# Out-of-range rows for the empty places of the order by destination in a four-layer graph network

## The reference, cut to what matters

```python
x = _layernorm(x + _L0_gnn_ref(x, edge_index, edge_weight, weights))  # 3 hops: segment_sum(w * z[dst], src), 4 matmuls
x = _layernorm(x + _L1_gnn_ref(...))  # 8 heads; keys and values by edge type; softmax over the edges of each dst
x = _layernorm(x + _L2_gnn_ref(...))  # 4 heads; leaky_relu(x_l[src] + x_r[dst]); softmax over the edges of each dst
x = _layernorm(x + _L3_gnn_ref(...))  # 8 heads; softmax over the edges of each src, then summed over each dst
```

## Time and profile before

| | us |
|---|---|
| median of 3 runs (lowest, highest) | 9730.03 (9727.62, 9735.21) |
| the profiled execution's own time | 9737.26 |
| its span in the trace | 9735.5 |
| POOL, DVE, PE, ACT busy | 6993.0, 6539.5, 6374.2, 2118.1 |
| mean granted clock of TensorE, share of full | 0.686 |

### The profile page before, as it was taken

One profiled execution on the slowest core, in us unless ns is written; L12 is line 12 of the kernel. 1 busy time (PEld: TensorE's weight loads), 2 busy tenths in 40 slices (PEclk: granted clock), 3 DMA queues, 4 the chain that ended last, 5 costly groups with the idle time before them and its releaser, 6 DMA issues. The chain is left out here.

```text
span 9735.5 us, 171552 instructions
## 1 busy us (share of the span) xinstructions
PE 6374.2 (65%) x37681; PEld 5551.4 (57%) x37682; DVE 6539.5 (67%) x22695; ACT 2118.1 (22%) x6216; POOL 6993.0 (72%) x7418
## 2 busy tenths in 40 slices
PE   6777655547666577639404666767776688876666
PEld 5666544436655566634204666556675578766665
DVE  7555566668777777736305888877777666667777
ACT  5222100001111111112101222232222222223333
POOL 7777777767777777777776777547775577767775
PEclk7555555556666655569756888889999665667777
DMA  0000012122212212234303333222222322223333
GB/s 25 2 2 2 18 53 52 53 61 53 53 53 55 57 53 53 53 77 146 100 2 86 104 104 104 87 47 55 55 55 55 100 54 54 54 72 108 108 108 97
DMA packets 436037, 614.74 MB, mean 63 GB/s; under 512 B 176561, under 2 KB 312069, under 8 KB 435109
## 3 DMA queue, kind: packets, MB, share of 16 engines
q0 software_dynamic: 257024, 486.93, 19.6%
q1 hardware_dynamic: 178305, 119.49, 4.3%
q10 hardware_dynamic: 292, 3.41, 0.1%
HBM read 520.17 MB, written 89.19 MB: 63 GB/s over the span
## 5 line engine op out<-in xcount | busy, mean ns | idle before, releaser
L1179 PE MATMUL hop_sums<-hop_rows,hop_weighted 128*128 x4992 | 1152.1, 403 | 1053.2 <-SPq L1315 674.4
L1128 POOL DMA_INDIRECT hop_rows<-hops,k_src_gather x1568 | 1483.3, 946 | 486.8 <-issue 477.6
L1179 PEld LDWEIGHTS hop_sums<-hop_rows,hop_weighted 128*128 128x128 f32 x4992 | 989.6, 295 | 1158.8 <-issue 1158.7
L1505 POOL DMA_INDIRECT l_pass_rows<-left_table,k_dst_other x832 | 796.2, 957 | 433.2 <-issue 244.6
L1505 POOL DMA_INDIRECT l_pass_rows<-related,k_dst_typed x832 | 788.6, 948 | 308.6 <-issue 238.7
L1505 POOL DMA_INDIRECT l_pass_rows<-key_table,k_src_gather x784 | 744.3, 949 | 365.9 <-issue 234.8
L2000 POOL DMA_INDIRECT l_weigh_rows<-row_table,l_weigh_ring x832 | 790.0, 949 | 297.9 <-issue 213.1
L728 POOL DMA_INDIRECT src_sorted<-src_scatter_records,src_scatter_places x784 | 753.1, 961 | 260.4 <-issue 188.2
L1355 POOL DMA_INDIRECT dst_sorted<-rec,dst_places x768 | 752.8, 980 | 237.2 <-issue 237.2
L1128 POOL DMA_INDIRECT hop_rows<-in_x,k_src_gather x784 | 742.4, 947 | 249.0 <-issue 238.7
L1213 DVE TENSOR_SCALAR hop_weighted<-k_numbers,k_src_place,src_weight 128x128 f32<-128x128 f32 x2496 | 850.1, 403 | 15.7 <-issue 8.7
(11 more groups left out here) (477 smaller groups left out, 17048.9 us busy)
## 6 DMA issues: line engine op xcount, KB each, us to landing
related<-l_tables_rows SPq DMA_DIRECT2D x50, 1024.0 KB, 4.5
hop_rows<-hops,k_src_gather POOLq DMA_INDIRECT x1568
l_pass_rows<-related,k_dst_typed POOLq DMA_INDIRECT x832
l_pass_rows<-left_table,k_dst_other POOLq DMA_INDIRECT x832
l_weigh_rows<-row_table,l_weigh_ring POOLq DMA_INDIRECT x832
src_sorted<-src_scatter_records,src_scatter_places POOLq DMA_INDIRECT x784, 2.1
hop_rows<-in_x,k_src_gather POOLq DMA_INDIRECT x784, 2.5
dst_sorted<-rec,dst_places POOLq DMA_INDIRECT x784
```

What stands on the lines that cost most here:

```text
L1128: nc.gpsimd.indirect_dma_start(rows[:, s * G + g, :], None, table_in, bass.IndirectOffsetOnAxis(ap=o.gather[:, c:c + 1], axis=0),).then_in ...
L1179: last = nc.tensor.matmul(sums[:, b, g, :], weighted[:, s % SLOTS, g, :], rows[:, bass.ds(slots[g], 1), :], start=True, stop=True)
L1505: nc.gpsimd.indirect_dma_start(rows[:, s, g, :], None, table, bass.IndirectOffsetOnAxis(ap=index[:, c:c + 1], axis=0),).then_inc(got[s], 16)
```

## The change

The records of "no edge" now name source `NO_NODE` = 6,271, a row behind the last node, and type 7. The gathers of the three stages carry a bound: an index greater than it is not an error, and its row is not transferred. The bound is 6,249 for layer 2 and weighing, and 7 x 6,400 + 6,249 for layer 1. The first gathers into each ring slot (the first 11, 15 and 4 groups) carry no bound and transfer all 128 rows, row 6,271 for the empty places; later an empty place keeps what the ring slot held. The 352 entries with source 0 and type 0 are below the bound and are transferred as before. The gathers of layer 3's softmax get the new argument too, with no bound. In weighing GpSimd's first round is written out ahead of a loop of 51.

```diff
-PAD_STEP, PAD_SKIP = 7, 3
-assert PAD_STEP * (CH - 1) + PAD_SKIP * (P - 1) < N
+NO_NODE = NP - 1
+assert NO_NODE >= N
@@ load_beside
-        nc.gpsimd.iota(pad[:, :, 1], [[PAD_STEP, CH]], base=0, channel_multiplier=PAD_SKIP,
-                       allow_small_or_imprecise_dtypes=True).then_inc(filled, 1)
         nc.gpsimd.memset(pad[:, :, 0:1], -1.0).then_inc(filled, 1)
-        nc.gpsimd.memset(pad[:, :, 2:4], 0.0).then_inc(filled, 1)
+        nc.gpsimd.memset(pad[:, :, 1:2], float(NO_NODE)).then_inc(filled, 1)
+        nc.gpsimd.memset(pad[:, :, 2:3], float(TYPES - 1)).then_inc(filled, 1)
+        nc.gpsimd.memset(pad[:, :, 3:4], 0.0).then_inc(filled, 1)
...
-        act.wait_ge(filled, 3)
+        act.wait_ge(filled, 4)
@@ softmax_pass(..., ringed=False, last_row=None)
                     nc.gpsimd.indirect_dma_start(rows[:, s, g, :], None, table,
                                                  bass.IndirectOffsetOnAxis(ap=index[:, c:c + 1], axis=0),
-                                                 ).then_inc(got[s], 16)
+                                                 bounds_check=last_row if n >= ring else None,
+                                                 oob_is_err=False).then_inc(got[s], 16)
@@ weigh_and_sum
-            with pool.Fori(0, ROUNDS) as i:
+            def a_round(i, first):
...
-                                                     ).then_inc(got[s], 16)
+                                                     bounds_check=None if first else N - 1,
+                                                     oob_is_err=False).then_inc(got[s], 16)
+
+            in_rounds(pool, ROUNDS, a_round)
@@ the calls
+ layer 1: last_row=(TYPES - 1) * NPD + N - 1
+ layer 2: last_row=N - 1
```

More of the change, by code:

```diff
@@ L1361, in softmax_pass @@
 def softmax_pass(nc, k, o, index, table, row, head, values_at, spread, att, peaks, total, reload, loops, wg, name, beside=(),
-                 ringed=False):
+                 ringed=False, last_row=None):
     heads = D // head
@@ L3266, in graph_network @@
             softmax_pass(nc, k, by_dst, by_dst.typed, related.rearrange("t n f -> (t n) f"), 2 * D, D // HEADS1, D,
-                         k.x, None, False, total, (k.x[:], x_home), None, 4, "l1_pass")
+                         k.x, None, False, total, (k.x[:], x_home), None, 4, "l1_pass", last_row=(TYPES - 1) * NPD + N - 1)
             relation_output(nc, k, total, a["L1_gnn_w_basis_a"], a["L1_gnn_loop_weight"], a["L1_gnn_bias"], mix,
@@ L3283, in graph_network @@
             softmax_pass(nc, k, by_dst, by_dst.other, left_table, D + HEADS2, D // HEADS2, 0, right, att_row[:], True, total,
-                         None, (left, loop_scores, k.x[:], bias2[:]), 8, "l2_pass")
+                         None, (left, loop_scores, k.x[:], bias2[:]), 8, "l2_pass", last_row=N - 1)
             attention_output(nc, k, total, loop_scores, left_table, "l2_out")
```

## The result

The changed kernel takes 9832.4 us (median of 4 runs, 9824.3 to 9838.7) against 9732.6 us for the kernel before in the same runs: ratio 1.0104, 95% interval 1.0092 to 1.0116. It is slower by 100 us. The profiled execution took 9838.7 us with a span of 9837.0, 101.5 us longer than before.

The account below looks back on a forecast made before the run. POOL's (GpSimd's) time per gather instruction, not bytes, was taken as the bound. Check cost less freed rows less waits gave +21.3 (layer 1), +45.4 (layer 2), +20.3 (weighing): +87 us, forecast 9817 us, range 9660 to 10,080.

Parts of the forecast that it names:

- The case: Forecast case: in the three bounded stages the check costs more than left-out rows free; 9817 us, chance 0.40.
- the bound on 2,376 gathers: Comparing 128 indices per bounded gather on POOL: 80.4 us in layer 1, 78.7 in layer 2, 83.2 in weighing.
- left-out rows: POOL time freed by rows not transferred: 22.4 us in layer 1, 22.1 in layer 2, 22.6 in weighing.
- POOL's idle time filled: POOL's present waits shrink before a stage grows: 36.7 us in layer 1, 11.2 in layer 2, 40.3 in weighing.
- I take 102 ns: Assumed extra POOL time per bounded gather, taken from the smallest memset, as one more pass over one column.
- 85 ns for one more read command: Alternative price per bounded gather if the core writing the other descriptors reads indices too; sum +46 us, not +87.
- I take half, 3.7 ns: Assumed POOL time freed per left-out row, half of its full share of 7.4 ns in a 949 ns gather.
- a pair of descriptors for each piece moved: Rule behind the rival of a free check and left-out rows freeing POOL time: 9649 or 9680 us, chance 0.32.
- less the wait of 36.7: Layer 1's sum: 80.4 less 22.4, less POOL's whole wait of 36.7 us for VectorE, gives +21.3 us.
- The prediction's case of 40 ns: At about 40 ns a gather, nothing freed, layer 1 and weighing hide the cost; layer 2 pays 20 us.
- Named signs: Expected in the changed profile: bounded gathers about 1,045 ns, last 22 shorter, POOL's waits near zero, VectorE's weighing wait above 191.4.
- The edits at nothing: Three memsets for the fill (1.6 us at most, covered) and weighing's written-out first round were said to cost nothing.

## Why the prediction was right

The forecast was 9817 in a range of 9660 to 10,080; 9832 came. The case was the right one, and its place too: POOL's gathers with a bound, three stages, nothing elsewhere. But each of its three terms had the wrong size, and the errors cancelled: that the time came within 16 us of the forecast is luck.

| us | predicted | measured |
|---|---|---|
| the bound on 2,376 gathers | +242.3 | +118.4 |
| left-out rows | -67.1 | 0 (none seen) |
| POOL's idle time filled | -88.2 | -20.5 |
| sum | +87.0 | +97.9 |

*The bound's price.* "I take 102 ns" was a choice by the nearest row, a small memset. The busy times grew by 39.2, 39.9 and 39.3 us, 50 ns for each of 2,376, and some 53 when the 3 ns of the profile before are allowed for. A memset over 128 words on POOL was a poor measure for a comparison inside another instruction: twice too high. The estimate from the Trainium skill's GPSIMD Engine Reference (section 7, Performance pitfalls for Q7 kernels), 85 ns for one more read command, was too high as well. Nothing here shows what the bound's price is made of.

*What a left-out row frees.* "I take half, 3.7 ns" failed entirely. Leaving all 128 out changes the median by nothing (998 and 998), and even asking for 64 rows fewer gives 0.73 ns a row. The packets stay, 48 a gather, when the bytes go. So the rule of the Trainium skill's page DMA: Bandwidth & Descriptors (SWDGE vs HWDGE vs iDMA), a pair of descriptors for each piece moved, is no guide to the time of a gather here.

*What the waits hide.* "less the wait of 36.7", 11.2 and 40.3 read a label as a duration. The earlier trace rows had the warning: a gap of 0.30 us is there also when it is put down to VectorE. A plain gap lasts 0.305 us on the mean (213.1 us of "issue" over 699 gaps in weighing). So the 75 waits of layer 1 hold 22.9 us of plain gap, the 31 of layer 2 hold 9.5 of 11.2, and the 132 of weighing behind the first hold all 40.3. What a slower POOL can fill is the idle time beyond one gap for each gather. 831 gaps are 253.3 us: of its 275.4 us of idle time layer 1 had 22.1 beyond them, layer 2 of 255.8 had 2.5, weighing of 253.4 next to nothing. Afterwards layer 1's idle time is 239.0 + 16.9 = 255.9: 19.5 less. The run with the bound in layer 1 alone shows it by itself. With the bound's measured price, nothing freed, and the prediction's own subtraction of the waits, the sum would have been 118.4 - 88.2 = +30 us: this reading matters as much as the price. The prediction's case of 40 ns said that weighing would hide all of it; weighing paid 39.3 us, in full.

*Named signs.* Means of about 1,045 ns: 995 to 1,005. The last 22 below their neighbours: they are not. POOL's waits near zero: 16.9, 17.6 and 2.8 are nearly all gaps. VectorE's wait for rows in weighing above 191.4: 242.0. The gap at 0.30, the move hidden: so it was. The edits at nothing cost nothing that the trace shows.

What the prediction did not see is the effect of the new empty places by themselves. The run with them alone shows at the stages' ends that gathers which all name one row are slow on the DMA engines. In the changed kernel the bound leaves out nearly all of those rows.

## What to carry to other kernels

Where GpSimd's issue of gathers is the bound, count instructions and not rows or bytes: in weighing a gather of 128 rows took 946 ns, of 64 rows 899, and one that moves nothing, with a bound, 998. Leaving rows out by an index past a bound lightens the DMA engines (0.40 to 0.03 of their time in weighing), so it could pay where they set the time, which no run here tried. It also avoids the slowness of many indices that name the same row; spreading those indices over the table does that at no cost (9732.6 us). And before a wait is taken as slack, subtract the gap that stands before every instruction of its kind.

## What was not expected of the hardware

- A bound on an indirect gather costs some 53 ns between medians (944 to 946 without, 997 or 998 with it; 49 or 50 against the profile before) in every stage that gathers, 14 ns more when an index above it is an error, and nothing for the register (29 ns, hidden in the gap of 0.30 us).
- A row past the bound keeps its packets: 257,024 in both kernels, 48 a gather with all rows left out; asking for 64 rows leaves 32.
- The rows of a gather hardly count: 899 ns for 64, 946 for 128, which is 0.73 ns a row and, if linear, about 850 ns fixed (an estimate).
- Gathers that read row 6,271 128 times are slow on the DMA engines: at the end of layer 2 the DMA engines were busy 0.76 of the time for 45 GB/s, where spread rows had taken 0.29 for 55.
- Open: what moves layer 3's softmax between 980 and 992 us, and what follows it between 45 and 58, among kernels that have the same code there.
